# Ranking the expert gates in two halves, and visiting every expert twice

## The chip, the core and the metric

The kernel runs on one core of a Trainium2 chip. The metric is the device time in microseconds of one execution, as the median of several. The engines are named as in the profile: PE (TensorE matmul), PEld (its weight loads), DVE (VectorE), ACT (ScalarE), POOL (GpSimd, which here also issues all indirect DMAs) and SP (SyncE, which issues most other DMAs).

## What is computed

A layer norm without weights, then attention with low-rank query and key projections and a causal mask, and beside it a mixture of experts in which each expert picks its tokens. Both are added to the input. The arrays are float32: 16 batches, 512 tokens, 256 channels; 16 heads of 16 channels; 8 experts with 512 hidden channels, each taking 128 tokens of every batch.

```
xn = layernorm(x)
q, k = (xn @ q_a) @ q_b, (xn @ k_a) @ k_b        # per head, rank 64
v = xn @ v_w.T + v_b
y = softmax(causal(q @ k.T / 4)) @ v @ o_w.T + o_b
probs = softmax(xn @ choice_w.T)                 # over the 8 experts
G, I = top_k(swap(probs), 128)                   # per batch and expert: 128 tokens
h = silu(xn[I] @ w1[e])
out = zeros.at[I].add(G * (h @ w2[e]))
result = x + y + out
```

## The kernel before

**Attention stage.** The work is cut into 64 slots, one for four heads of one batch (`G = 4*b + g`), each of ten units `t`. `slot_steps` writes down, for a slot, which steps stand at which unit; every engine walks the same list in the same order and does its own part of each step, waiting on semaphores. A slot computes `score` of slot G+3 (PE, then a row maximum on DVE, line 719), `scoret` of slot G+1 (PE, `exp` on ACT line 565, causal mask on POOL line 469) and `pv` of slot G (PE line 908; the copy `yraw` on ACT line 569 comes once per slot, so its start marks the slots). `PROJECTIONS` puts the work for later batches between them: `xload` and `lnstat` (the load of `xln`, then its statistics on DVE, line 657), `xt`, `qk` and `mid` (projections, split into three bf16 parts on ACT, DVE line 588 `rest` and POOL, then stacked by twelve DMAs of SP for the scores of the batch two later), `v`, `o`, and `xres` (SP loads x again into `xres`, POOL adds the bias, line 477). Pairs of batches 1 to 6 run in a hardware loop, the first and last pair stand as straight code.

**Routing.** `routing_steps` puts the gates at the end. When the logits of all 16 batches are there (slot 56), DVE and ACT make the softmax of [128, 4, 16, 8] values; PE transposes them, so that 128 partitions are the pairs (batch, expert) with 512 tokens each. Then DVE draws the 128 largest of each row by 47 operations in a chain (`RANK_OPS`: `max` of eight, `max_index`, `match_replace`; lines 633 to 637), 5 to 8 of them in each of slots 57 to 63. `rows` turns the places into row numbers, `rowst` transposes back, and POOL gathers the tokens of the first two groups by eight indirect DMAs. Scratch for this lies in `xn` and `xln`, free by then.

**Expert stage.** It is a second block of instructions, begun when all engines have ended the first. A group is one expert and four batches (`GB4`); there are 32 groups `n = 4*e + grp`, and the weights of an expert are loaded and split into a high and a low part once (`w` on ACT line 1070, `w_low` on DVE line 1089). A group is: gather of 4 x 128 rows (POOL line 961), `pick` (PE transposes, split on ACT and DVE line 1094), `h` (PE line 1141, silu on ACT line 1078, split on DVE lines 1098 and 1100), `down` (PE line 1157, product with the gate on DVE line 1109 into `mixed`), and four scatter-adds into the output (POOL line 1049). POOL's order is gather of group n+2, scatter of group n-1, gather of group n+3, and so on; the scatter of a group waits until that of the group four back has landed.

## Time and profile before

| | |
|---|---|
| Time, 3 runs | 1301.11, 1294.84, 1301.05 us; median 1301.05 |
| Profiled execution, its own time | 1295.71 us |
| Its span in the trace | 1293.8 us |
| Mean granted TensorE clock | 0.969 |
| Busy: PE, DVE, POOL, ACT | 1184.1, 967.2, 692.0, 668.7 us |
| Attention stage | 0 to 861 us |
| Expert stage | 861 to 1294 us |

Busy times are sums over both stages, which have different limits. A matmul's end is modelled, so a PE that is always busy is not PE at its peak. A row of the timeline gives the start, the duration, the engine and line, and in brackets how long the engine was idle before and what it then waited for.

### The profile page before, as it was taken

How to read it: one execution, taken by the hardware profiler on the slowest of the kernel's cores; microseconds unless marked ns; L12 is line 12 of the kernel's file. 1: busy time of each engine (PE TensorE's matmuls, PEld its weight loads, DVE VectorE, ACT ScalarE, POOL GpSimd, SP SyncE). 2: the span in 40 equal slices, each digit the busy share in tenths (PEclk: the TensorE clock that was granted, in tenths of full speed). 3: DMA queues.
4: the chain of work that ended last, by engine and by line, in shares of the span. 5: the costliest groups of instructions: out<-in, count | busy, mean ns of one | idle time of the engine just before them, and what ended most of it. 6: DMA issues, size and time to landing. Idle time of an engine off the chain costs nothing. (4 is left out here: it accounts for less than half of the span.)

```text
span 1293.8 us, 29459 instructions
## 1 busy us (share of the span) xinstructions
PE 1184.1 (92%) x8502; PEld 819.8 (63%) x8502; DVE 967.2 (75%) x3293; ACT 668.7 (52%) x1312; POOL 692.0 (53%) x1021
## 2 busy tenths in 40 slices
PE   6799999999999999999999998769999999999995
PEld 5545555555555555555555553348988888888885
DVE  3588888879889888888888879935666666666662
ACT  2357667667667677677667665522332323233320
POOL 1235344355355355345345443344888888888885
PEclk9779999999999999999999999979999999999998
DMA  5443443443443443443444342132555555556454
GB/s 141 114 116 83 116 116 100 116 116 98 115 115 98 115 115 99 115 115 100 113 115 112 100 99 67 34 114 38 111 99 95 114 93 102 94 100 109 85 78 53
DMA packets 106287, 130.31 MB, mean 101 GB/s; under 512 B 21580, under 2 KB 75476, under 8 KB 106196
## 3 DMA queue, kind: packets, MB, share of 16 engines
q1 hardware_dynamic: 76356, 94.46, 28.1%
q0 software_dynamic: 24576, 33.57, 15.6%
q10 hardware_dynamic: 5264, 1.32, 0.5%
q8 instruction: 27, 0.44, 0.1%
q14 instruction: 64, 0.52, 0.1%
HBM read 44.84 MB, written 33.55 MB: 61 GB/s over the span
## 5 line engine op out<-in xcount | busy, mean ns | idle before, releaser
L719 DVE CUSTOM_DVE_ANT_0 junk<-bank,rowmask 128x256 bf16<-128x256 f32 (+3 forms) x1024 | 454.9, 485 | 60.3 <-PE bank L866 38.0
L565 ACT ACTIVATE probs<-bank 128x512 f32<-128x512 f32 x640 | 377.3, 598 | 158.0 <-PE bank L887 143.8
L469 POOL TENSOR_SCALAR_AFFINE_SELECT probs<-probs 128x256 f32<-128x256 f32 (+1 forms) x640 | 224.2, 363 | 311.0 <-ACT probs L565 308.9
L866 PE MATMUL bank<-kstk,qstk 96*128 96x256 bf16 (+3 forms) x1024 | 250.7, 306 | 34.3 <-DVE rowmax L719 17.3
L887 PE MATMUL bank<-qstk,kstk 98*128 98x256 bf16 (+3 forms) x1024 | 251.0, 307 | 3.8 <-ACT probs L565 2.6
L1049 POOL DMA_INDIRECT out_rows<-mixed,rows x128 | 208.9, 1632 | 58.2 <-issue 38.1
L1078 ACT ACTIVATE hid<-bank 128x512 f32<-128x512 f32 x128 | 76.6, 598 | 228.5 <-PE bank L1141 228.5
L908 PE MATMUL bank<-probs,vaug 128*32 128x512 f32 (+3 forms) x2048 | 168.5, 448 | 6.6 <-POOL probs L469 6.6
L1157 PE MATMUL bank<-w_hi,hid_hi 128*128 128x256 f32 x512 | 147.3, 288 | 0.0
L1157 PE MATMUL bank<-w_hi,hid_lo 128*128 128x256 f32 x512 | 144.9, 283 | 0.0
L1157 PE MATMUL bank<-w_lo,hid_hi 128*128 128x256 f32 x512 | 144.8, 283 | 0.0
L866 PEld LDWEIGHTS bank<-kstk,qstk 96*128 96x128 bf16 x1024 | 89.7, 100 | 79.5 <-DVE rowmax L719 38.3
L887 PEld LDWEIGHTS bank<-qstk,kstk 98*128 98x128 bf16 x1024 | 76.7, 99 | 99.2 <-issue 48.0
L1109 DVE TENSOR_SCALAR mixed<-bank,gate_sel 128x256 f32<-128x256 f32 x128 | 56.1, 480 | 92.0 <-PE bank L1157 92.0
L908 PEld LDWEIGHTS bank<-probs,vaug 128*32 128x32 f32 x2048 | 54.1, 110 | 95.9 <-issue 74.1
L460 POOL TENSOR_TENSOR qk_part<-rest,qk_part 128x512 bf16<-128x512 f32 x64 | 74.6, 1166 | 58.0 <-ACT qk_part L541 55.1
L1157 PEld LDWEIGHTS bank<-w_lo,hid_hi 128*128 128x128 f32 x512 | 98.2, 192 | 0.0
L1157 PEld LDWEIGHTS bank<-w_hi,hid_hi 128*128 128x128 f32 x512 | 98.2, 192 | 0.0
L1157 PEld LDWEIGHTS bank<-w_hi,hid_lo 128*128 128x128 f32 x512 | 98.1, 192 | 0.0
L1098 DVE CAST hid_hi<-hid 128x512 fp32r<-128x512 f32 x128 | 56.9, 445 | 48.7 <-ACT hid L1078 47.1
L1100 DVE TENSOR_TENSOR hid_lo<-hid,hid_hi 128x512 fp32r<-128x512 f32 x128 | 89.2, 697 | 4.4
L719 DVE DVE_READ_ACCUMULATOR2_ANT rowmax<- 128x1 f32 x1024 | 84.8, 83 | 0.0
(131 smaller groups left out, 2097.8 us busy)
## 6 DMA issues: line engine op xcount, KB each, us to landing
qstk<-qk_part SPq DMA_DIRECT2D x96, 256.0 KB, 4.8
kstk<-qk_part SPq DMA_DIRECT2D x96, 256.0 KB, 4.7
xln<-in_L_attn_hidden_states SPq DMA_DIRECT2D x16, 512.0 KB, 6.1
xn_rows<-xn SPq DMA_DIRECT2D x16, 512.0 KB, 2.8
xres<-in_L_attn_hidden_states SPq DMA_DIRECT2D x16, 512.0 KB, 3.6
out_rows<-xres SPq DMA_DIRECT2D x16, 512.0 KB, 2.9
qstk<-in_L_ffn_w SPq DMA_DIRECT2D x8, 512.0 KB, 4.0
kstk<-in_L_ffn_w SPq DMA_DIRECT2D x8, 512.0 KB, 3.9
```

The costliest lines, as they stand in the source:

```text
L460: nc.gpsimd.tensor_tensor(qk_part[2][:, k, :], rest[k % 2][:], qk_part[1][:, k, :], ALU.subtract).then_inc(lo_done, 1)
L469: nc.gpsimd.affine_select(out=block, in_=block, compare_op=ALU.is_ge, fill=0.0, base=0, pattern=[[0, len(cols)], [1, P]], channel_multipli ...
L565: nc.scalar.activation(probs[n % 2][:, 512 * k:512 * k + 512], SCORET[k % 2][:], ACT.Exp, scale=SCALE).then_inc(exp_done, 1)
L719: last = nc.vector.tensor_tensor_reduce(out=junk[k % 2][:, col:col + width], in0=SCORE[score_bank(UN * n + k)][:, col:col + width], in1=ro ...
L866: last = nc.tensor.matmul(SCORE[score_bank(UN * n + k)][:, col:col + width], qstk[b % 2][0:KS, GH * g + h, P * i:P * i + P], kstk[b % 2][0 ...
L887: last = nc.tensor.matmul(SCORET[k % 2][:, col:col + width], kstk[b % 2][0:KS + SHIFT, GH * g + h, P * j:P * j + P], qstk[b % 2][0:KS + SH ...
L908: last = nc.tensor.matmul(Y[2 * HD * h:2 * HD * h + 2 * HD, P * k:T], vaug[b % 2][:, k, GH * g + h, :], probs[n % 2][:, col:col + width], ...
L1049: nc.gpsimd.indirect_dma_start(out=out_rows, out_offset=bass.IndirectOffsetOnAxis(ap=moe.rows[:, GB4 * grp + j, e:e + 1], axis=0), in_=mix ...
L1078: nc.scalar.activation(hid[k % 2][:], UP[k][:], ACT.Silu).then_inc(silu_done, 1)
L1098: nc.vector.tensor_copy(hid_hi[n % 2][:, k, :], hid[k % 2][:]).then_inc(hid_high, 1)
L1100: nc.vector.tensor_tensor(hid_lo[n % 2][:, k, :], hid[k % 2][:], hid_hi[n % 2][:, k, :], ALU.subtract).then_inc(hid_done, 1)
L1157: last = nc.tensor.matmul(DOWN[k][:, D * t:D * t + D], a, b, start=m == 0, stop=m == len(todo_mm) - 1)
```

## The change

The gates are ranked in two halves of eight batches. For the first half, softmax, transpose and ranking stand in slots 28 to 55, two ranking operations in each of slots 30 to 53 (at units 2 and 4), on 64 partitions of 512 tokens. The second half has its softmax and transpose in slots 57 and 58, and its 47 ranking operations go into the expert stage: four in each of the first twelve groups. The scratch has tiles of its own.

An expert is now visited once for each half, with two groups at a visit: 16 visits, each of which loads and splits the expert's weights. A scatter waits for the one two groups back. The gathers of the first two groups are issued by POOL in slots 59 to 61 (`fetch`). The bias add on POOL becomes a step of its own (`xadd`), in the same place but for the last batch, where it stands after the last causal masks. Only the second and third pair of batches still run as a loop; the rest, and DVE and SP in the expert stage, stand as straight code.

```diff
+PER_VISIT = HB // GB4
+VISITS = 2 * E
+LOOPED = 3
...
-RANK_PLACES = {7: (4, 5, 6, 8, 9), 6: (0, 1, 3, 4, 6, 7), 5: (0, 1, 3, 4, 6, 7), 4: (0, 1, 3, 4, 6, 7),
-               3: range(8), 2: range(8), 1: range(8)}
+RANK_PLACES = (2, 4)
+RANK_FIRST = 30
...
+    for half, gates in enumerate((28, NG - 7)):
+        if G == gates:
+            out += [(5, ("gate_max", half, 0)), (6, ("gate_max", half, 1)), (7, ("gate_exp", half, 0)),
+                    (8, ("gate_norm", half, 0)), (9, ("gate_norm", half, 1))]
+        if G == gates + 1:
+            out += [(0, ("gate_norm", half, 2)), (2, ("rankt", half, 0))]
...
+    done = len(RANK_PLACES) * (G - RANK_FIRST)
+    if 0 <= done < RANK_OPS:
+        out += [(t, ("rank", done + m, 0)) for m, t in enumerate(RANK_PLACES) if done + m < RANK_OPS]
...
+    if 3 <= NG - G <= 5:
+        first = 3 * (5 - (NG - G))
+        out += [(t, ("fetch", *divmod(first + m, GB4))) for m, t in enumerate((1, 4, 7)) if first + m < 2 * GB4]
...
-    return [("yt", B - 1, 0), ("rowst", 0, 0), ("gather", 0, 0), ("gather", 1, 0), ("yt", B - 1, 1)] \
+    return [("xadd", B - 1, 0), ("yt", B - 1, 0), ("gather", 0, 0), ("gather", 1, 0), ("yt", B - 1, 1)] \
...
+def expert_steps(body):
...
+        n = EG * body + grp
+        v, second = divmod(n, PER_VISIT)
+        if n == RANK_GROUPS:
+            out.append(("rowst", 1, 0))
         out += [("h", n, ft) for ft in range(FT)]
+        if second and v + 1 < VISITS:
+            out += [("w", v + 1, 0), ("w_low", v + 1, 0)]
...
+        out += [("rank", n, 0)] * (n < RANK_GROUPS)
+        for j in range(GB4 // 2):
+            out += [("down", n - 1, j)] * (n >= 1) + [("rank", n, 1)] * (n < RANK_GROUPS and j == 0)
+        if n == RANK_GROUPS - 1:
+            out.append(("rows", 1, 0))
+        if not second and v >= 1:
+            out += [("w", v, 1), ("w_low", v, 1)]
...
+def place_of(n):
+    v, second = divmod(n, PER_VISIT)
+    half, e = divmod(v, E)
+    return HB * half + GB4 * second, e
```

Where instructions stand, engine by engine. DVE in the attention stage, the second slot of a batch, before (`stats` is the last `lnstat`, `junk,rowmax` are pieces of the row maxima of `score`):

```order
L657 BN_STATS stats<-xln 128x6 x2
L663 BN_AGGR meanvar<-stats 128x2 x4
L719 ISA junk,rowmax<-bank,rowmask 128x256
L719 ISA rowmax 128x1
L719 ISA junk,rowmax<-bank,rowmask 128x256
L719 ISA rowmax 128x1
L756 TENSOR_TENSOR xres<-bank,xres 128x256
L719 ISA junk,rowmax<-bank,rowmask 128x512
```

And the same place of the changed kernel, in a slot from 30 to 53:

```order
L729 ISA junk,rowmax<-bank,rowmask 128x256
L729 ISA rowmax 128x1
L766 TENSOR_TENSOR xres<-bank,xres 128x256
L1004 MAX top<-ranked 64x8
L729 ISA junk,rowmax<-bank,rowmask 128x512
L729 ISA rowmax 128x1
L729 ISA junk,rowmax<-bank,rowmask 128x384
L729 ISA rowmax 128x1
L729 ISA junk,rowmax<-bank,rowmask 128x128
L729 ISA rowmax 128x1
L1006 MAX_INDEX top_at<-top,ranked 64x8
```

Two ranking operations now stand between the row maxima of each of these slots; nothing else moved there.

POOL at the end of the attention stage, before (`probs` are causal masks, `xres` the bias add of the last batch, the DMAs the first gathers):

```order
L477 TENSOR_TENSOR xres<-xres,ob_all 128x1024
L469 AFFINE_SELECT probs<-probs 128x2x128
L469 AFFINE_SELECT probs<-probs 128x128
L469 AFFINE_SELECT probs<-probs 128x2x128
L469 AFFINE_SELECT probs<-probs 128x128
L469 AFFINE_SELECT probs<-probs 128x2x128 x2
L469 AFFINE_SELECT probs<-probs 128x128
L469 AFFINE_SELECT probs<-probs 128x2x128
L961 DMA qstk<-xn_rows,rows 128x256 x4
L961 DMA kstk<-xn_rows,rows 128x256 x4
```

And after (the last of the eight single gathers, in slot 61, down to the end of the stage):

```order
L988 DMA kstk<-xn_rows,rows 128x256
L486 AFFINE_SELECT probs<-probs 128x128
L486 AFFINE_SELECT probs<-probs 128x2x128 x2
...
L486 AFFINE_SELECT probs<-probs 128x128
L486 AFFINE_SELECT probs<-probs 128x2x128
L494 TENSOR_TENSOR xres<-xres,ob_all 128x1024
```

The last bias add went behind the last masks, and the gathers went two slots forward.

DVE in the expert stage, before, a group behind which the next expert's `w1` is split:

```order
L1089 TENSOR_TENSOR w_lo<-qstk,w_hi 128x1024
L1093 REGISTER_ALU
L1094 TENSOR_TENSOR pt_lo<-bank,pt_hi 128x512
L1093 REGISTER_ALU
L1094 TENSOR_TENSOR pt_lo<-bank,pt_hi 128x512
L970 ISA
L970 COPY gate_sel<-gates 128x4
L1104 REGISTER_ALU
L1109 TENSOR_SCALAR mixed<-bank,gate_sel 128x256 x4
```

And after, the first such group:

```order
L1135 TENSOR_TENSOR w_lo<-qstk,w_hi 128x1024
L1158 TENSOR_TENSOR pt_lo<-bank,pt_hi 128x512 x2
L996 COPY gate_sel<-gates 128x4
L1006 MAX_INDEX top_at<-top,ranked 64x8
L1007 MATCH_REPLACE ranked<-top,ranked 64x512
L1173 TENSOR_SCALAR mixed<-bank,gate_sel 128x256 x2
L1004 MAX top<-ranked 64x8
L1006 MAX_INDEX top_at<-top,ranked 64x8
L1173 TENSOR_SCALAR mixed<-bank,gate_sel 128x256 x2
```

Two ranking operations stand ahead of each half of `mixed`, and such a group with a `w_lo` now comes every second time instead of every fourth.

## Rows read from the trace of the kernel before

**Rows 1.** The page: busy sums, and POOL's 40 slices in tenths.

```profile
PE 1184.1 (92%) x8502; PEld 819.8 (63%) x8502; DVE 967.2 (75%) x3293; ACT 668.7 (52%) x1312; POOL 692.0 (53%) x1021
POOL 1235344355355355345345443344888888888885
```

**Rows 2.** The page: the chain that ended last, by engine.

```profile
POOL 23%; issue 6%; PE 3%; DMA 0%; DVE 0%; ACT 0%; POOLq 0%
```

**Rows 3.** Busy by window, expert stage: PE, PEld, DVE, ACT, POOL, then clock, DMA.

```profile
888.00:1263.00 375.00, 358.46 (x2339) 322.08 (x2338) 239.51 (x450) 113.78 (x188) 305.43 (x229) 1.00 0.54 97
```

**Rows 4.** Busy by window, one batch in mid attention: two slots, one, one.

```profile
604.30:629.40 25.10, 23.37 (x186) 13.86 (x185) 20.17 (x84) 17.08 (x39) 10.30 (x23) 1.00 0.62 143
629.40:640.50 11.10, 11.03 (x96) 7.07 (x97) 10.74 (x46) 7.41 (x14) 2.50 (x7) 1.00 0.37 121
640.50:652.00 11.50, 11.50 (x85) 6.25 (x84) 10.08 (x42) 8.47 (x17) 9.08 (x17) 1.00 0.10 30
```

**Rows 5.** Timeline of DVE where a batch turns over.

```profile
609.92 0.69 DVE L588 TENSOR_TENSOR rest<-bank,qk_part 128x512 f32<-128x512 f32 x1
623.41 0.43 DVE L657 BATCH_NORM_STATS2 stats<-xln 128x6 f32<-128x256 f32 x1 [2.07 <-DMA xln<-in_L_attn_hidden_states]
657.70 0.69 DVE L588 TENSOR_TENSOR rest<-bank,qk_part 128x512 f32<-128x512 f32 x1
```

**Rows 6.** Busy by window: the two parts of that batch's turn.

```profile
609.90:623.40 13.50, 11.85 (x99) 7.24 (x98) 9.94 (x40) 9.11 (x22) 5.03 (x12) 1.00 0.71 165
623.40:657.70 34.30, 34.15 (x269) 20.01 (x269) 31.11 (x130) 23.94 (x47) 16.86 (x35) 1.00 0.33 91
```

**Rows 7.** Timeline of DVE: a value load; a MAX8 and its follower.

```profile
824.79 0.08 DVE L635 MATCH_VALUE_LOAD xn<-xn,xln 128x8 f32 x1
...
827.07 0.69 DVE L633 MAX8 xn<-xln 128x8 f32<-128x512 f32 x1
827.67 0.41 DVE L756 TENSOR_TENSOR xres<-bank,xres 128x256 f32<-128x256 f32 x1
```

**Rows 8.** Busy by window: slots 56 and 57; 58 and 59; 60; 61 to 63.

```profile
747.50:775.30 27.80, 25.68 (x190) 14.27 (x188) 21.54 (x86) 18.09 (x40) 9.73 (x22) 0.94 0.48 111
775.30:801.10 25.80, 21.38 (x157) 9.70 (x158) 24.84 (x97) 13.08 (x25) 9.17 (x21) 0.93 0.26 84
801.10:813.10 12.00, 9.11 (x74) 4.19 (x75) 11.72 (x48) 6.98 (x14) 3.90 (x11) 1.00 0.01 2
813.10:843.60 30.50, 22.47 (x183) 10.84 (x181) 26.22 (x76) 15.73 (x29) 10.71 (x25) 0.89 0.11 36
```

**Rows 9.** Busy by window of line 776 alone (`qk`): PE, PEld; two slots.

```profile
629.40:652.00 22.60, 4.94 (x15) 2.61 (x15) 1.00 0.23 75
```

**Rows 10.** Timeline of the handover, 831 to 861 us, single rows.

```profile
834.81 2.35 POOL L477 TENSOR_TENSOR xres<-xres,ob_all 128x1024 f32<-128x1024 f32 x1 [5.39 <-ACT probs L565]
839.75 3.80 PE L908 MATMUL bank<-probs,vaug 128*32 128x512 f32 x32 [5.13 <-POOL probs L469]
855.11 0.38 SPq L412 DMA_DIRECT2D out_rows<-xres  x1
857.39 0.94 POOL L961 DMA_INDIRECT kstk<-xn_rows,rows  x1 [0.30 <-issue]
860.85 1.94 PE L1125 MATMUL bank<-ident,qstk 128*128 128x128 f32 x8 [6.37 <-PEq L218]
```

**Rows 11.** Timeline of POOL and DVE where an expert's weights are split.

```profile
1027.25 1.02 POOL L961 DMA_INDIRECT qstk<-xn_rows,rows  x1 [0.30 <-issue]
...
1029.30 1.23 DVE L1089 TENSOR_TENSOR w_lo<-kstk,w_hi 128x1024 fp32r<-128x1024 f32 x1 [0.28 <-ACT w_hi L1070]
1029.87 1.48 POOL L961 DMA_INDIRECT qstk<-xn_rows,rows  x1 [0.30 <-issue]
...
1040.88 1.02 POOL L961 DMA_INDIRECT kstk<-xn_rows,rows  x1 [0.30 <-issue]
...
1053.55 1.02 POOL L961 DMA_INDIRECT qstk<-xn_rows,rows  x1 [0.31 <-issue]
```

More of the change, by code:

```diff
@@ L158, in __init__ @@
         self.out_stored = out_stored
+        self.ranked = ranked
+        self.top = top
+        self.top_row = top_row
+        self.top_at = top_at
+        self.first = first
 def build(nc, x, q_a, q_b, k_a, k_b, v_w, v_b, o_w, o_b, choice_w, w1, w2, out):
@@ L174, in build @@
     U_PAIR, S_PAIR = 48, 16
-    for i in range(1, PAIRS - 2):
+    for i in range(1, LOOPED - 1):
         for s, z in zip(pair_steps(i), pair_steps(i + 1)):
@@ L213, in build @@
             gathered=[sem(f"gathered{g}") for g in range(EG)],
-            out_stored=sem("out_stored"))
+            out_stored=sem("out_stored"),
+            ranked=[keep(f"ranked{u}", [HALF, T], fp32) for u in range(2)],
+            top=keep("top", [HALF, CAP], fp32), top_row=keep("top_row", [HALF, CAP], fp32),
+            top_at=keep("top_at", [HALF, CAP], u32), first=keep("first", [P, 1], fp32))
         banks = [ctx.enter_context(nc.psum_tensor(f"bank{i}", [P, 512], fp32)) for i in range(8)]
@@ L304, in build @@
             out_stored = moe.out_stored
-            gate_step = sem("gate_step")
+            gate_step = [sem(f"gate_step{half}") for half in range(2)]
             bias_step = sem("bias_step")
@@ L947, in expert_steps @@
             out += [("pick", n + 1, dt) for dt in range(DT)]
-        if n + 2 < E * EG:
+        if n + 2 < EG * E:
             out.append(("gather", n + 2, 0))
-        if n >= 1:
-            out += [("down", n - 1, j) for j in range(GB4 // 2)]
-        if grp == 0 and e >= 1:
-            out += [("w", e, 1), ("w_low", e, 1)]
-    return out + [("down", n, j) for j in range(GB4 // 2) if e == E - 1]
-def gather(nc, moe, xn_dram, n):
-    e, grp = divmod(n, EG)
-    for j in range(GB4):
-        nc.gpsimd.indirect_dma_start(
-            out=moe.picked[grp][:, j, :], out_offset=None, in_=xn_dram,
-            in_offset=bass.IndirectOffsetOnAxis(ap=moe.rows[:, GB4 * grp + j, e:e + 1], axis=0)).then_inc(moe.gathered[grp], 16)
@@ new lines, in expert_steps, with gather, select @@
+    return out + [("down", n, j) for j in range(GB4 // 2) if body == E - 1]
+def place_of(n):
+    v, second = divmod(n, PER_VISIT)
+    half, e = divmod(v, E)
+    return HB * half + GB4 * second, e
+def gather(nc, moe, xn_dram, n, j):
+    first, e = place_of(n)
+    nc.gpsimd.indirect_dma_start(
+        out=moe.picked[n % EG][:, j, :], out_offset=None, in_=xn_dram,
+        in_offset=bass.IndirectOffsetOnAxis(ap=moe.rows[:, first + j, e:e + 1], axis=0)).then_inc(moe.gathered[n % EG], 16)
+def select(nc, moe, n):
+    first, e = place_of(n)
+    nc.vector.tensor_copy(moe.gate_sel[n % EG][:], moe.gates[:, first:first + GB4, e:e + 1]).then_inc(moe.sel_done, 1)
@@ L973, in experts, with rank, by_be @@
+def rank(nc, moe, n):
+    r, op = divmod(n, 3)
+    a, z, eight = moe.ranked[r % 2], moe.ranked[(r + 1) % 2], slice(8 * r, 8 * r + 8)
+    if op == 0:
+        return nc.vector.max(moe.top[:, eight], a[:])
+    if op == 1:
+        return nc.vector.max_index(moe.top_at[:, eight], moe.top[:, eight], a[:])
+    return nc.vector.match_replace(z[:], moe.top[:, eight], a[:], -1.0)
+def by_be(t, half):
+    return t[:, HB * half:HB * half + HB, :].rearrange("p b e -> p (b e)")
 def experts(nc, sem, ident, banks, moe, xn_dram, out_rows):
@@ L1005, in experts, with whole @@
         added = [sem(f"added{g}") for g in range(EG)]
+        rank_step, rows_ready, rows_in, gates_in = sem("rank_step"), sem("rows_ready"), sem("rows_in"), sem("gates_in")
+        same = lambda value, per_body: value
+        def whole(steps_fn):
+            steps_fn(start_steps + [s for body in range(E) for s in expert_steps(body)], same)
         def program(eng, steps_fn):
-            same = lambda value, per_expert: value
+            turn = RANK_GROUPS // EG
             steps_fn(start_steps + expert_steps(0), same)
-            with eng.Fori(1, E - 1) as e:
-                steps_fn(expert_steps(1), lambda value, per_expert: e * per_expert + (value - per_expert))
+            with eng.Fori(1, turn) as i:
+                steps_fn(expert_steps(1), lambda value, per_body: i * per_body + (value - per_body))
+            steps_fn(expert_steps(turn), same)
+            with eng.Fori(turn + 1, E - 1) as i:
+                steps_fn(expert_steps(turn + 1), lambda value, per_body: i * per_body + (value - (turn + 1) * per_body))
             steps_fn(expert_steps(E - 1), same)
```

229 lines of the change are left out of this document (117 added, 112 removed), and 2 rows, old and new, of the table PROJECTIONS.

## The prediction

> **What bounds the kernel now.** I read the page first. Its busy sums call PE the bound, at 92%, but they are averages over two stages. The slices of POOL in [rows 1] show the two: half busy or less in the attention stage, 8 tenths in all of the expert stage. The chain that ended last names POOL with 23% and "issue" with 6% of the span in [rows 2].
>
> The windows of the expert stage settle it. From 888 to 1263 us POOL is busy 305.4 of 375.0 us with 229 instructions [rows 3]. Each has about 0.3 us of issue ahead of it [rows 11], 229 x 0.3 = 68.7 us, and 305.4 + 68.7 = 374.1. POOL never waits there. A group costs it four gathers and four scatters, about 13 us, so this stage is as long as POOL's list, counted from the first scatter.
>
> In the attention stage I read windows cut at the slots. One batch takes 25.1 + 11.1 + 11.5 = 47.7 us, of which PE is busy 45.9 and DVE 41.0; in the third slot DVE has 0.4 us to spare, in the fourth 1.4 [rows 4]. The timeline shows a turn of fixed length in it: from the last `rest` of a batch at 609.92 to the statistics at 623.41, which waited 2.07 us for the load of `xln` queued behind the stacking DMAs, is 13.5 us; from there to the next such `rest` at 657.70 is 34.3 us [rows 5]. In the 34.3 us DVE is busy 31.1, so it has 3.2 us of idle time; in the 13.5 us it is busy 9.9 [rows 6].
>
> The end of the attention stage is bound by DVE, with the ranking: 24.8 busy of 25.8 us in slots 58 and 59, 11.7 of 12.0 in slot 60 [rows 8]. After that comes a handover in which little runs: the bias add on POOL at 834.81, after a wait of 5.39 us, holds the last masks, and with them PE for 5.13 us; the gathers need the finished ranking, so the last is issued at 857.39 and the expert stage's first matmul starts at 860.85 [rows 10].
>
> **The change part by part.** The sum is made against the profiled execution's own time, 1295.7 us (span 1293.8, about 2 us around it). The median of the runs shown is 1301.05; I carry the difference over to that.
>
> (a) *Ranking leaves slots 57 to 63: -19 us.* What would these slots take without it? Slots 58 and 59 belong to a batch with no projections for a later one. The pair of slots that answers to them takes 11.1 + 11.5 = 22.6 us with PE full [rows 4], and 4.94 us of it are the 15 `qk` matmuls that fall away [rows 9]: 17.7. DVE's 20.8 us of work there lose the `rest` and `xn` pieces too, so it is no tighter. Against 25.8 now [rows 8] that is -8.1. Slot 60 is 12.0 and would be some 9.7 with the next batch's projections gone: -2.3. Slots 61 to 63 have no scores; they now take 30.5 together (the last of it held up by the bias add, whose wait is gone because it stands behind the masks) and I take 24.5: -6.0. Slots 56 and 57 take 27.8 now against a normal 25.1; they lose some projections and keep half of the softmax, so I take 25.0: -2.8. Sum -19.2. The bounds are -11, where the slots stay at the length of normal ones, and -24. The eight fetches lie on POOL at slots 59 to 61: 8 x 1.25 = 10 us (0.94 and 0.3 of issue [rows 10]) on an engine busy 9.2 of 25.8 us [rows 8]. Behind a fetch wait the masks, and behind these `pv`; a mask of 0.3 to 0.4 us comes about once in 1 us, so a delay of 1.25 is worked off within two. I cost them at nothing, at worst 3.
>
> (b) *Handover: -5 us.* The block ends with its slowest engine, now POOL at 858.33; 2.5 us later PE starts. Without the gathers the last is SP's issue of the final store at 855.11 [rows 10], so -3; the transposes and copies of `rowst` in between, and PE's lowered clock (0.89 on average from 813 to 844 [rows 8], where it waited for POOL) give perhaps 2 more, with 1 to 5 as bounds. The first groups may also see the full clock sooner, for which I take -1.5, an estimate between 0 and 3.
>
> (c) *First half's ranking in slots 30 to 53: +12 us.* A ranking operation put between others costs 0.60 us (a MAX8, from its start to that of its follower), and the two other kinds 0.08 more for their value load [rows 7]: 0.65 on average, on all partitions or half of them alike, since time goes by the 512 tokens. Two per slot are 1.3 us. Six of the 24 slots fall in the 13.5 us stretches, where DVE waits 2.07 us for the load anyway: hidden, and if that cover were gone, 8 us. The other 18 add 18 x 1.3 = 23.4 us to the stretches of 34.3 us, six in number, with 3.2 us of idle each, 19.2 in all. If all of it can be used the cost is 4; if none, 23. Slots 58 to 60 show that DVE can run with 2 to 4% idle [rows 8], 1.2 us of 37, so 2 us a stretch are usable: 23.4 - 12 = 11.4. PE is nearly full in the stretches, which it is not in slots 58 to 60; I take 12. Behind DVE wait PE's next scores (three banks) and the shared banks of the projections.
>
> (d) *First half's softmax in slots 28 and 29: +1.5.* Five operations of half size and a transpose; bounds 0.5 and 4.
>
> (e) *Eight more visits: +5.5 us.* PE and ACT have the room. POOL has none. Where the low part of `w1` is made on DVE (1.23 us), the gather under it takes 1.48 us instead of 1.02, and POOL's group is 13.6 us long (1027.25 to 1040.88) where the next is 12.7 (to 1053.55) [rows 11]. Part of that 0.9 is the place in the pattern; at 0.7 each, 8 x 0.7 = 5.5; bounds 0 and 8. The scatter's wait for the one two groups back has a whole group's POOL time between, some 13 us, against a landing of 2 to 4: no cost.
>
> The Trainium skill, SBUF — State Buffer, section "Who interferes with whom", has it that a DVE operation with two SBUF inputs competes only with GpSimd's reads and, by inference there, not with the writing of descriptors. By that rule this term would be 0. The row speaks against it.
>
> (f) *Second half's ranking in twelve groups: +1; first scatter later: +2.* DVE is busy 239.5 of 375 us [rows 3], 8.3 of 13 per group. Four operations are 2.6 us, the second split every other group 0.6 more: 11.5 of 13. POOL stays the bound, and what DVE delays is hidden behind its list, except before the first scatter, where a split (1.2) and two to four ranking operations now stand ahead of the first `mixed`.
>
> (g) *Straight code instead of loops: 0.* Slots of the first pair, which is straight code today, last as long as those in the loop; the extra wait at the loop's end is taken out of the wait for the load in [rows 5].
>
> Sum: -19.2 - 5 - 1.5 + 12 + 1.5 + 5.5 + 3 = -3.7 us. From 1295.7 that is 1292.0; from the median, 1297.
>
> **The rivals.** *Better hidden (chance 0.26).* The ranking in mid attention fills DVE's idle time almost whole: (c) is 5 rather than 12, the change -11, time 1290. For it: DVE ran 98% full in slot 60. Against: PE is full there as well, and DVE's idle time lies late in the stretch.
>
> *No cost of splits (0.10).* The lengthened gather is due to the weight's DMA or to chance, (e) is 0, and the change is -9.2: 1292. The rule of the Trainium skill named above would give this. The boundary in [rows 11] repeats at the other experts, so I hold it unlikely.
>
> *DVE sets the pace in mid attention (0.17), the one on the other side.* No idle time is usable, since in-order PE stalls on the shared banks as soon as DVE lags; (c) is 23 and the change is +7: 1308. It is slower than before as soon as (c) is over 16.
>
> *The expert stage becomes DVE's (0.07).* In a group with a split, the last `hid_lo` of PE's `h` is followed on DVE by 1.2 + 1.4 + 0.2 + 2.6 + 1.8 = 7.2 us, after 5.4 of `h`: 12.6 beside POOL's 12.9. If waits add 1 us to each of twelve groups: +12 - 3.7 = +8, 1309.
>
> *The end doesn't shrink (0.05).* Masks and `pv` hold slots 58 to 63 near their present length, (a) is -11: +4.5, 1305.
>
> That leaves 0.35 for the forecast itself, with a range of its own of 1292 to 1302.
>
> **How the numbers follow.** What a measurement can tell from no change is about 0.5%, 6.5 us. Faster than 1294.5 are the first two rivals, 0.36. Slower than 1307.6: the third and fourth but for a part of each, 0.20. Within: 0.44. The range goes to the better-hidden case with a larger (a) below, and to the case on the other side above: 1283 to 1311.
>
> **What would show it.** Windows over four slots between 30 and 53: 49.7 us a batch by (c) (48.5 if well hidden, 51.5 if not), DVE over 95% busy. Slots 58 and 59: 17 to 18 us together. From the last `yraw` to the first `pick` about 12 us. The expert stage from first matmul to the end: 441 us against 433 now, with POOL still without waits, and gathers of 1.4 us at every second group. I would be wrong if POOL waited for `mixed` there, or if the slots with ranking took over 13 us each.

## The result, and the profile after

The changed kernel takes 1318.91 us in the median of 4 runs (1313.63 to 1322.76), the kernel before 1297.94 beside it (4 runs): a ratio of 1.016, with an interval of 1.011 to 1.021. It is slower, and by more than the range of the forecast allowed. The profiled execution has a span of 1311.9 us (own time 1313.6).

The page of the changed kernel: busy sums, PE's granted clock in 40 slices, the packets that bring code (the queue named `instruction`; 0.92 MB in 56 packets are 16 KB each), and the group in which PE waits for the stacking DMAs.

```profile
PE 1190.9 (91%) x8508; PEld 822.1 (63%) x8508; DVE 1010.2 (77%) x3396; ACT 686.4 (52%) x1330; POOL 696.9 (53%) x1021
PEclk9879999999999999998999999989999999999998
q8 instruction: 56, 0.92, 0.3%
L877 PE MATMUL bank<-kstk,qstk 96*128 96x256 bf16 (+3 forms) x1024 | 254.6, 311 | 39.1 <-DMA kstk<-qk_part 30.1
```

The same page of the kernel before has this row of code packets:

```profile
q8 instruction: 27, 0.44, 0.1%
```

To see where the time went I compared the starts of the `yraw` copies, one per slot, of both traces. At the copy of slot 55 the changed kernel is 35.0 us behind (first row before, second after). By slot 63 it has won 14.0 back, by the first `pick` of the expert stage another 6.1, it loses 0.4 until the first scatter and 2.8 from there to the last: 35.0 - 14.0 - 6.1 + 0.4 + 2.8 = 18.1, the difference of the spans. So the end and the handover shrank by 20.1 of the 25.7 us that I had for them, and mid attention cost 35 us where 13.5 stood in the sum.

```profile
747.52 0.60 ACT L569 ACTIVATE yraw<-bank 128x512 f32<-128x512 f32 x1 [0.44 <-PE bank L908]
782.53 0.60 ACT L587 ACTIVATE yraw<-bank 128x512 f32<-128x512 f32 x1 [0.44 <-PE bank L919]
```

Of the 35.0 us, 5.9 had come by slot 27, 3.8 came in slots 28 and 29, where the first half's softmax stands, and 25.4 in slots 30 to 55.

I call the stretch from the last `rest` of a batch to the statistics its turn, as in [rows 5], and number it by the batch, counted from 0, whose pieces are stacked in it. The turn of batch 12, which answers to [rows 6], by windows: from the statistics to the last `rest`, from there to the next statistics (the turn), and the 3.4 us from just before its end; then slots 56 and 57, 58 and 59, 60, and 61 to 63, as in [rows 8]. The columns are those of [rows 3].

```profile
595.27:633.63 38.36, 37.33 (x272) 20.88 (x272) 34.49 (x140) 24.19 (x47) 16.93 (x35) 0.94 0.30 81
633.63:648.43 14.80, 12.13 (x100) 7.48 (x99) 10.80 (x45) 9.20 (x22) 5.02 (x12) 0.98 0.67 153
648.00:651.40 3.40, 3.40 (x18) 1.49 (x21) 2.83 (x12) 1.65 (x4) 0.41 (x1) 0.52 0.00 0
...
782.50:809.30 26.80, 24.84 (x186) 14.25 (x185) 18.72 (x78) 17.32 (x38) 9.23 (x22) 0.94 0.49 109
809.30:831.50 22.20, 19.45 (x161) 9.95 (x162) 18.58 (x81) 13.38 (x26) 10.32 (x22) 1.00 0.34 103
831.50:840.40 8.90, 8.57 (x74) 4.05 (x73) 8.34 (x38) 6.73 (x13) 6.37 (x14) 1.00 0.17 49
840.40:864.60 24.20, 20.62 (x183) 10.72 (x182) 7.83 (x29) 15.43 (x29) 15.03 (x30) 1.00 0.21 66
```

Both parts of the batch grew: 38.4 us against 34.3 and 14.8 against 13.5 [rows 6]. DVE is not full, it idles 3.9 of the 38.4 us, so it is not the rival in which DVE sets the pace. And the clock stands at 0.52, the lower of its two levels (1.2 GHz), for those 3.4 us. Ahead of that PE had waited for the stacking DMA, on PE's timeline:

```profile
647.10 0.38 PE L877 MATMUL bank<-kstk,qstk 96*128 96x512 bf16 x1 [2.55 <-DMA kstk<-qk_part]
```

In the kernel before this wait is 1.5 us in every other batch and nothing in the rest (only the weight load ahead waits, 0.2 to 0.4 us), with no fall of the clock from 338 to 768 us. The changed kernel has waits of 1.8 to 3.0 us in the eight turns of batches 7 to 14 and nine falls, one in each batch from 388 to 801 us.

### The profile page after: what moved, and what is told of

It is laid out like the page before. It is cut to its first block and busy times, and to the rows that moved or that the text cites. A ratio compares the mean times of both kernels' runs of the same rounds, so it can differ in the third digit from the quotient of the medians.

```text
span 1311.9 us, 27293 instructions
## 1 busy us (share of the span) xinstructions
PE 1190.9 (91%) x8508; PEld 822.1 (63%) x8508; DVE 1010.2 (77%) x3396; ACT 686.4 (52%) x1330; POOL 696.9 (53%) x1021
## 5 line engine op out<-in xcount | busy, mean ns | idle before, releaser
L729 DVE CUSTOM_DVE_ANT_0 junk<-bank,rowmask 128x256 bf16<-128x256 f32 (+3 forms) x1024 | 453.7, 483 | 47.8 <-PE bank L877 39.5
L877 PE MATMUL bank<-kstk,qstk 96*128 96x256 bf16 (+3 forms) x1024 | 254.6, 311 | 39.1 <-DMA kstk<-qk_part 30.1
L898 PE MATMUL bank<-qstk,kstk 98*128 98x256 bf16 (+3 forms) x1024 | 255.3, 312 | 4.2 <-DMA qstk<-maxrow 2.4
L988 POOL DMA_INDIRECT qstk<-xn_rows,rows x64 | 69.9, 1092 | 30.9 <-issue 18.1
L1213 PE MATMUL bank<-pt_hi,w_hi 128*128 128x512 f32 x256 | 80.5, 396 | 4.0 <-DVE pt_lo L1158 4.0
```

What stands on the lines that cost most here:

```text
L729: last = nc.vector.tensor_tensor_reduce(out=junk[k % 2][:, col:col + width], in0=SCORE[score_bank(UN * n + k)][:, col:col + width], in1=ro ...
L877: last = nc.tensor.matmul(SCORE[score_bank(UN * n + k)][:, col:col + width], qstk[b % 2][0:KS, GH * g + h, P * i:P * i + P], kstk[b % 2][0 ...
L898: last = nc.tensor.matmul(SCORET[k % 2][:, col:col + width], kstk[b % 2][0:KS + SHIFT, GH * g + h, P * j:P * j + P], qstk[b % 2][0:KS + SH ...
L988: nc.gpsimd.indirect_dma_start(out=moe.picked[n % EG][:, j, :], out_offset=None, in_=xn_dram, in_offset=bass.IndirectOffsetOnAxis(ap=moe.r ...
L1213: last = nc.tensor.matmul(UP[k][:], a[:, dt, f], b[:, dt, :], start=m == 0 and dt == 0, stop=m == 2 and dt == DT - 1)
```

## The experiments

Two things of the change touch every batch in mid attention: the ranking on DVE, and the code, written out where there was a loop. The packets of code doubled. The first runs take these two apart.

**Code alone.** The kernel before, with the loop of the attention stage kept for pairs 1 and 2 only.

```diff
-                with eng.Fori(1, PAIRS - 1) as i:
+                with eng.Fori(1, LOOPED) as i:
...
-                steps_fn(pair_steps(PAIRS - 1) + epilogue_steps(), same)
+                steps_fn([s for i in range(LOOPED, PAIRS) for s in pair_steps(i)] + epilogue_steps(), same)
```

> The kernel before with one edit: only pairs 1 and 2 of the attention run as a loop, the rest is straight code, as in the changed kernel; no other instruction is added or moved. If straight code is a cause (theory S: the code that must be fetched delays the last stacking DMAs, PE's wait for them grows from 1.5 to about 2.6 us, and its clock then halves for 3.4 us), the turn from the last rest to the statistics is 14.3 us or more instead of 13.5 in batches 7 to 13, a batch takes 50 to 50.5 us instead of 47.8, and the time is 12 to 20 us longer. If the ranking alone is the cause (theory R), the time is within 4 us of before and the turn stays 13.5 us.

Measured: 1312.88 us, ratio 1.012 (1.009 to 1.016). Written-out code costs 16 us with nothing else changed; the run has 50 packets of 16 KB instead of 27 (an expectation below says 29 more, which is the changed kernel's number). The turns of batches 7, 9, 10, 11 and 14 grew and their last transfer came late (batch 8's grew too, 14.9 us, with a packet 11.4 us in and the last transfer in time); those of 12 and 13, which I had expected to grow too, did not. Two batches of this run, by windows; they do the same work:

```profile
623.50:671.30 47.80, 45.44 (x362) 26.70 (x362) 40.40 (x166) 32.70 (x68) 21.95 (x47) 1.00 0.44 112
522.80:573.00 50.20, 47.00 (x356) 27.06 (x355) 39.46 (x161) 32.07 (x66) 20.66 (x46) 0.93 0.38 97
```

The first is as short as a batch of the looped kernel, so written-out code isn't slow in every batch. What differs is a packet. These are the DMA queues from 4 to 12 us into the turn, in the slow batch (526.8 to 534.8 us) and, behind the dots, in the good one (627.5 to 635.5), and PE's wait behind each:

```profile
q1 hardware_dynamic: 1050, 1.76, 98.4%
q8 instruction: 1, 0.02, 1.1%
q10 hardware_dynamic: 34, 0.01, 0.7%
...
q1 hardware_dynamic: 1079, 1.79, 100.3%
q10 hardware_dynamic: 34, 0.01, 0.7%
```

```profile
536.65 0.58 PE L867 MATMUL bank<-kstk,qstk 96*128 96x512 bf16 x1 [2.92 <-DMA kstk<-qk_part]
...
635.89 0.38 PE L867 MATMUL bank<-kstk,qstk 96*128 96x512 bf16 x1 [1.52 <-DMA kstk<-qk_part]
```

**Load alone.** The loop kept, and two MAX8 of 64x512 that nothing depends on in each of slots 8 to 55.

```diff
+    if 8 <= G < 56:
+        for t in (2, 4):
+            put[t].append(("load", G, t))
...
+                        elif kind == "load":
+                            nc.vector.max(spare[:, 8 * (k // 4):8 * (k // 4) + 8], rowmask[0:64, :])
```

> The kernel before, with two MAX8 of 64 x 512 put into units 2 and 4 of each of slots 8 to 55, on DVE, of data that nothing else uses; the loop stays. They stand for the ranking operations, 1.2 us a slot. Theory R (DVE's load alone lengthens the turn and brings the clock down): a batch takes over 50 us and the time is 25 us longer or more over 12 batches. Theory S: the turn stays 13.5 us, the loop's clock stays 1.0, and each batch is longer only by what DVE cannot hide, 1.5 to 2.5 us, in all 18 to 30 us; the turn from rest to statistics tells the two apart.

Measured: 1314.67, ratio 1.016 (1.014 to 1.018). The two parts of a batch:

```profile
584.67:621.04 36.37, 35.43 (x276) 20.47 (x275) 34.29 (x136) 24.58 (x48) 17.39 (x36) 1.00 0.32 86
621.04:634.23 13.19, 11.47 (x96) 6.95 (x95) 10.94 (x42) 8.85 (x21) 5.04 (x12) 1.00 0.70 164
```

Eight operations of 0.6 us make a batch 1.5 us longer, 49.4 instead of 47.8 on average over slots 16 to 51, in the part ahead of the turn; the turn is no longer, and the clock doesn't fall. By the whole time, 19.6 us in twelve batches, it is 1.6. For the six batches of the real ranking that is 9 to 10 us.

**Both.** Written-out code, and the same load in slots 30 to 53.

> The kernel before with both edits: straight code from pair 3 on, and two MAX8 in each of slots 30 to 53. It is the changed kernel's mid attention without its other parts. If straight code and load explain the loss there, the 55th yraw starts 30 to 36 us later than in the kernel before, and e1 gives what of it is the code. If it is later by under 20, something else of the change (the softmax in slot 28, the tiles' places) takes the rest.

Measured: 1317.41, ratio 1.017 (1.014 to 1.020). From code alone it is 4.5 us, about half of 9. That the whole time is the change's own is chance, for this run hasn't the 20 us that the change wins behind slot 55. Its copy of slot 55 starts 19.5 us behind the kernel before, where the changed kernel is 35.0 behind:

```profile
766.97 0.60 ACT L574 ACTIVATE yraw<-bank 128x512 f32<-128x512 f32 x1 [0.44 <-PE bank L915]
```

This is under the 20 that I had set as the mark, so code and load give 19.5 of the 35.0 us and something else of the change goes with 15.5. By stretches: 3.0 against 5.9 up to slot 27, 0.7 against 3.8 in slots 28 and 29, so that the softmax costs some 3 us, and 15.7 against 25.4 from slot 30 on. There the traces differ in where the packets fall: this run has four late turns (batches 7, 9, 10, 11) with four falls of the clock, the changed kernel six with nine. Its turns without a packet are longer too (below). How much each of these takes of the 9.7 us isn't told apart.

**The clock.** The changed kernel, with 8 matmuls that nothing reads ahead of PE's wait for the stacking DMAs (from batch 7 on, in a free score bank).

```diff
+                            if g == 0 and k == 0 and n >= 24:
+                                for _ in range(8):
+                                    nc.tensor.matmul(SCORE[score_bank(UN * n + k)][:], wqk_hi[:, 0, 0:P], wqk_hi[:, 0, :],
+                                                     start=True, stop=True)
                             if g == 0 and k == 0:
                                 pe.wait_ge(stacked[b % 2],
```

> The changed kernel, with eight matmuls of 512 columns (1.8 us) on PE ahead of its wait for the stacking DMAs, once for each batch from 7 on, into the score bank that is free then; their results are overwritten. If the length of PE's idle wait is what brings the clock down, the clock stays 1.0 through slots 28 to 60 and each of the eight batches is 1.5 us or so shorter: 10 to 14 us in all, near 1303. If the clock falls for another reason, or the wait is not what costs, the time stays within 3 us of the changed kernel or grows.

Measured: 1306.48, 12.4 us less than the changed kernel's median. Each against its own runs of the kernel before, ratios of 1.010 (1.007 to 1.013) and 1.016, it is some 8, so I take 8 to 12. From 380 to 780 us its clock is 1.00 (first row), that of the changed kernel 0.96 (second):

```profile
380.00:780.00 400.00, 384.78 (x2968) 228.28 (x2966) 352.29 (x1429) 265.06 (x546) 175.19 (x374) 1.00 0.43 106
380.00:780.00 400.00, 371.32 (x2806) 215.10 (x2805) 343.82 (x1390) 256.70 (x524) 169.63 (x361) 0.96 0.41 102
```

The turns stayed at 13.8 to 15.0 us, so the falls of the clock are a cost beside the late transfers, some 0.9 to 1.4 us for each of the nine. The same 8 matmuls in the written-out kernel before:

> The kernel before with all code written out, and 8 matmuls of 512 columns into a free score bank ahead of PE's wait for the stacking transfers, from slot 24 on, so that PE does not idle there. It parts the cost of written-out code (1.2%, 16 us) into the falls of the clock and the rest. Theory F: four falls in mid attention at 1.5 us each, as the same matmuls gave back some 12 us for eight or nine falls in the changed kernel: -5 to -7 us against the first experiment, a clock without falls between 340 and 780 us; the last transfers stay late by 1 us in the same turns. Rival K (the clock carries all of it): -14 us or more, back to the kernel before.

Measured: 1304.99 (ratio 1.006, 1.004 to 1.008), 7.9 us less than code alone. Half of the cost of the code is the clock. Late transfers are a large part of the rest: in the profiled run of code alone the turns of batches 7 to 14 sum to 113.7 us against 108.2 before, and each batch with a late turn is longer by some 2 us or more. The parting isn't clean, since the added matmuls moved the packets as well: here eight turns of batches 4 to 14 are late instead of five.

**Which engine's code.** Code written out on one engine, the loop kept on the others.

```diff
+                if eng in (nc.vector,):
+                    steps_fn([s for i in range(1, PAIRS) for s in pair_steps(i)] + epilogue_steps(), same)
+                    return
```

> The kernel before, with VectorE's code alone written out for all pairs of batches and the loop kept on the other engines. With all engines written out the median rose by 1.2%, and 29 more instruction packets came in mid attention. Theory F (a packet of code that is fetched while the stacking transfers run delays the last of these; PE's wait grows from 1.5 to some 2.6 us; the clock falls to half for 3.4 us after it): the packets are those of all engines together, so VectorE alone brings a part of them (some 10, by its share of the rows written out), the turns without a packet stay at 13.5 us, and the time rises by 2 to 6 us. Rival V (written-out code costs where VectorE itself runs it, whatever is fetched): nearly the whole 16 us come back. Rival P (it costs where PE runs it): 0.

> The kernel before, with PE's code alone written out for all pairs and the loop kept on the other engines. Theory F: PE has the most instructions, so most of the 29 added packets are its own, the turn is 14 us or more in those batches where a packet falls among the stacking transfers and 13.5 in the others, each of the former with a fall of the clock and some 3 us; +6 to +14 us in all. Rival V (VectorE's own written-out code costs): 0. Rival P (it costs where PE runs it, in all batches alike): +12 to +16 us spread evenly, with no falls of the clock.

Measured: 1300.86 for VectorE (ratio 1.005, 1.003 to 1.007), 1307.89 for PE (1.008, 1.006 to 1.011). Together they are some 18 us, about the whole. The added 16 KB packets are PE's: its run has 56, that of VectorE 27 as before. What VectorE's run changed are the 8 KB packets of another queue, q14, in their places, and to 46 from 64 rather than, as I had expected, to more of them. In PE's run the turns of batches 9, 11, 13 and 14 land late, at 13.5 to 13.9 us, with packets 4.5 to 5.9 us into the turn, and the other seven of batches 4 to 14 at 12.3 to 12.5. Only the last of the four has a fall of the clock, where I had expected one in each: so a late transfer costs without it, some 2 us in each of those batches. In VectorE's run two of these eleven turns had a packet of q14 among the stacking transfers (7.7 and 7.8 us into the turn), and only these two landed late, at 13.2 and 13.4 us.

**Moving the packets.** Is the packet the cause, or only there? The written-out kernel before, and 64 matmuls of 32 columns on PE ahead of a score, which shift all later packets.

```diff
+                            if n == 16 and k == 0:
+                                for _ in range(64):
+                                    nc.tensor.matmul(SCORE[score_bank(UN * n + k)][:, 0:32], wqk_hi[:, 0, 0:P], wqk_hi[:, 0, 0:32],
+                                                     start=True, stop=True)
```

> The kernel before with all code written out (as the first experiment), and 64 matmuls of 32 columns more on PE ahead of the scores of slot 16, which nothing reads. They are some 128 instructions of PE, half of the 256 that a 16 KB packet of code holds, so all later packets of PE's code come half a period, about 8 us, earlier beside the work. Theory F (a packet fetched in the stacking turn delays the last stacking transfer and PE): in the run without them the turns of batches 9, 10 and 11 had a packet 10 us into the turn and their last transfer landed after 13.1 to 13.7 us instead of 12.3. With the shift these three go back to 12.4 us, and batches 12 and 13, whose packets came just after the turn, at 12.5 to 13.5 us, get them at 4 to 6 us and land after 13 us or more. Rival C (the long turns belong to these places of the written-out code for another reason, such as the order of the semaphores or the batches' data): batches 9 to 11 stay late and 12 and 13 stay at 12.3. The time in all stays within 5 us of the first experiment's 1312.9.

Measured: 1323.91. The place lies in a step that the remaining loop runs twice, and the matmuls cost 21 us there, so the total says nothing. The turns do. The packets came 7 to 11 us earlier. Those of batches 10, 12 and 13 came 2 to 3 us into the turn, before the transfers; I had expected the last two at 4 to 6 us, and that half of the expectation wasn't tested. The last transfers of batches 7, 10, 11 and 14 went from 13.2 to 13.7 us to 12.3 to 12.5, batch 9 stayed at 13.0 with an 8 KB packet of q14 7.5 us into its turn. PE's wait in batch 10, 2.92 us above:

```profile
552.21 0.38 PE L871 MATMUL bank<-kstk,qstk 96*128 96x512 bf16 x1 [1.55 <-DMA kstk<-qk_part]
```

From slot 33 to slot 55 code alone had lost 9.4 us to the looped kernel; this run loses 0.6. The same shift in the changed kernel, placed where PE waits for its first data, in two sizes:

```diff
                 pe.wait_ge(ident_done, 1)
+                pe.wait_ge(consts, 3)
+                for _ in range(64):
+                    nc.tensor.matmul(SCORE[0][:, 0:8], ident_bf[:], ident_bf[:, 0:8], start=True, stop=True)
```

> The changed kernel, with 64 matmuls of 8 columns (bf16) at PE's very beginning, where it otherwise waits for its first data until 8 us; nothing reads them. They are 128 instructions, half of a 16 KB packet of code, and do nothing else but shift where the packets of PE's code fall in the slots: some 8 us earlier. In the changed kernel's trace a packet came 7 to 10 us into the turn in batches 7 to 12, the last stacking transfer landed after 13.3 to 13.8 us, and the clock fell once in every batch. Theory F: with the shift these packets come at about 1.5 us into the turn, before the transfers, the last lands after 12.7 us, most of the falls are gone, and the kernel is 8 to 14 us faster than the changed one (some 1306 to 1311). Rival C (written-out code and the ranking are slow there whatever the packets do): the changed kernel's 1318.9, within 3 us.

> The same with 32 matmuls in place of 64: a shift of some 4 us. Theory F: the packets that came at 7 to 10 us into the turn come at 3 to 6 us, still among the stacking transfers, and those of batches 13 and 14, which came at 13.1 us, come at 9; so all eight turns are late, and the time is the changed kernel's 1318.9 or up to 4 us more. Rival C: the same as with 64. Rival W (any matmuls at the start help, by the clock or by the order of things): as fast as with 64.

Measured: 1308.87 with 64 (ratio to the kernel before 1.011, 1.009 to 1.012), 1320.58 with 32 (1.019, 1.017 to 1.021). So 64 matmuls without use win 10 us by the medians and 7 by the ratios, and 32 win nothing; between the two runs, measured beside each other, are 11.7 us. With 32 the trace has slots 30 to 55 1.6 us shorter than in the changed kernel but reaches slot 7 5.9 us later (with 64: 5.4 shorter and 4.0 later), for which I have no reason. With 64 no packet of PE's is left among the transfers of batches 7 to 14 and seven of these eight turns land at 12.6 to 12.8 us; the eighth, 13.3, has a packet of q14. With 32 the shift was larger than I had reckoned: four turns have their packet at 2.4 to 2.9 us and are good, and the other four, with packets at 6.5 to 10.2 (one of them of q14), late. One step failed: with 64 the clock still fell in each of batches 9 to 14 of the profiled run (which, with 1316.1 us, was the slowest of the five), behind waits of 1.8 to 2.5 us, such as this one, with no packet from 1.9 to 12.0 us into the turn:

```profile
643.75 0.38 PE L880 MATMUL bank<-kstk,qstk 96*128 96x512 bf16 x1 [2.00 <-DMA kstk<-qk_part]
```

Over all 17 traces there are 187 turns (batches 4 to 14). In 42 a code packet starts 6.2 to 10.7 us into the turn: their last transfer lands after 13.0 us or more. In 135 none starts from 3.9 to 10.7 us: all land at 12.0 to 12.9 but one, 13.3, whose packet came at 3.8. The 10 between (3.9 to 6.2 us) are of both kinds. These bounds I drew after seeing the turns; the runs that moved the packets are the test, the count is not.

**A loop for the others.** The changed kernel, with pairs 4 and 5 as a loop on all engines but DVE.

> The changed kernel, with slots 32 to 47 (batches 8 to 11) as a loop of two turns on all engines but VectorE, where the ranking makes the two turns differ. The other engines have the loop's code by its second turn, batches 10 and 11. Theory F: in batches 10 and 11 few packets of code come, the turn falls from 14.7 to 13.6 us, the clock holds, and the two batches are 49 us long instead of 51; batches 8, 9 and 12 to 14 stay as they were. In all -3 to -7 us against the changed kernel. Rival R (the ranking itself lengthens the turn and the wait): batches 10 and 11 stay at 51 us, 0 in all.

Measured: 1316.58, the changed kernel's time within its spread. The loop's second round holds the turns of batches 12 and 13. They had no packet of PE's among the transfers and landed at 12.8, as in theory F, but were 14.7 and 14.0 us long instead of 13.6, one with a fall of the clock, and the two batches took 52.7 and 51.0 us, not 49. And in the turn of batch 11, where the loop goes round, POOL stood for 6.4 us and ACT for 3.4 with nothing that the trace shows as a cause:

```profile
587.32 0.29 POOL L492 TENSOR_SCALAR_AFFINE_SELECT probs<-probs 128x128 f32<-128x128 f32 x1 [6.37 <-issue]
```

**The bias add alone.** The kernel before, with `xadd` of the last batch at the start of the epilogue.

> The kernel before, with only the bias add of the last batch moved on GpSimd from slot 61 to behind the last causal masks, as in the changed kernel. In the kernel before PE waited 5.13 us for masks that stood behind this add, and the end of the attention stage needs the ranking as well, which lies on VectorE. If the wait of PE was on the path: -3 to -5 us from slot 63 on, of which the handover may take back the time of the add itself (some 2 us), because the store needs it. If the ranking on VectorE alone sets the end: 0.

Measured: 1290.27, ratio 0.997 (0.995 to 0.999): PE's wait of 5.13 us [rows 10] is 1.31, and this one edit gives 4 to 5 us, a fifth to a quarter of the 20 that the end and the handover gave the change.

```profile
829.77 2.37 POOL L477 TENSOR_TENSOR xres<-xres,ob_all 128x1024 f32<-128x1024 f32 x1
829.86 3.95 PE L908 MATMUL bank<-probs,vaug 128*32 128x512 f32 x32 [1.31 <-POOL probs L469]
```

**The splits.** The kernel before, and a subtraction of the size of a split in the second group of each expert.

```diff
+        out += [("spare", n, 0)] * (grp == 1)
...
+                    if kind == "spare":
+                        nc.vector.tensor_tensor(spare[:], w_hi[0][:], w_lo[0][:], ALU.subtract)
```

> The kernel before, and in the second group of each of the eight experts one more subtraction of the size of a low half of w1 on VectorE, of two tiles of SBUF into a third that nothing reads. My forecast had 0.7 us for each such subtraction, by the gathers beside it that take 1.48 instead of 1.02 us. If so: +5.6 us (0.4%), with a gather of some 1.4 us in each such group. By the changed kernel's own trace, where the expert stage grew by 2.8 us after its first scatter: +2.5 to +3. By the rule that such operations don't touch the writing of descriptors: 0.

Measured: 1294.78, ratio 0.9995 (0.998 to 1.001): nothing. But it fell beside scatters, which take 1.73 us there against 1.62 on average elsewhere, and not beside gathers, so it didn't test the row that the forecast went by.

**What stands against the kernel before.** `xadd` moved, and matmuls without use where PE idles between the stages.

```diff
+                            if n == B - 1 and k == 0:
+                                idle_matmuls(5)
...
                 program(pe, steps)
+                idle_matmuls(20)
...
+                            if n in (0, 1):
+                                for _ in range((5, 8)[n]):
+                                    nc.tensor.matmul(DOWN[0][:], w1_hi[:, 0, 0:P], w1_hi[:, 0, :], start=True, stop=True)
```

> The kernel before with the bias add of the last batch moved behind the last masks (1290.3 us, -0.33%, by itself), and matmuls that nothing reads where PE idles between the stages: 5 ahead of the last output projection, 20 behind it, 5 and 8 ahead of the first two groups' first layer. In the trace PE's clock is at half in 836 to 843 and 846 to 860 us, where the output projection takes 4.4 us instead of some 3 and the first group's first layer 8 instead of 5.6. If the clock stays at full: another -3 to -4 us, 1287. If POOL's gathers set the start and the first groups of POOL's list hide the rest: 0 to -1.

Measured: 1286.71, ratio 0.993 (0.991 to 0.995), faster than both kernels. From the last `yraw` to the first scatter the clock is 0.92 (first row), where it is 0.77 with `xadd` alone, and the stretch is 3.9 us shorter:

```profile
834.70:875.60 40.90, 35.09 (x184) 28.45 (x185) 23.75 (x50) 12.76 (x20) 16.65 (x17) 0.92 0.28 90
833.90:878.70 44.80, 30.36 (x146) 25.48 (x147) 22.34 (x46) 12.98 (x20) 15.37 (x16) 0.77 0.27 82
```

The changed kernel with all of these edits:

> The changed kernel with everything that the runs so far gave: the 64 matmuls at the start, 8 ahead of PE's wait for the stacking transfers from batch 7 on (they gave back 12 us), and those between the stages (they gave 3.6 us in the kernel before). If the three add up: 1318.9 - 12 - 6 - 3 = 1298; the first two share the falls of the clock, so the second gives only the transfers' 1 us in some six turns. Theory F has 1296 to 1300, so the halves still don't beat the kernel before, 1295, because the ranking in mid attention costs 1.5 us per batch in six batches and the lasting rest is 1 us or so per written-out batch. If the halves were good once the packets are out of the way: under 1291.

Measured: 1312.69 (1305.63 to 1321.88, ratio 1.012, 1.006 to 1.019). They don't add up; even its fastest run is behind the kernel before, so theory F's 1296 to 1300 missed. With the clock held in batches 7 to 14 and one late turn of these eight left, slots 30 to 55 still take 16.8 us more than before, of which the load is 9 to 10. In the profiled run, 1318.6 us, PE stood for 5.1 us where the first loop goes round:

```profile
284.81 0.61 PE L909 MATMUL bank<-qstk,kstk 98*128 98x512 bf16 x1 [5.08 <-issue]
```

## Why the prediction was wrong

(g) *Straight code: 0.* This step failed. It was argued from slots of the first pair lasting as long as looped ones. That reading was wrong: the two turns in that straight code (batches 2 and 3, at 126 and 176 us) take 14.1 and 13.8 us against 13.5 in the loop, and PE waits 2.1 and 1.9 us there against 1.5, the first time with a fall of the clock at 139.6. None of the rows in front showed it, the trace did:

```profile
139.24 0.38 PE L866 MATMUL bank<-kstk,qstk 96*128 96x512 bf16 x1 [2.14 <-DMA kstk<-qk_part]
```

Straight code costs 16 us in the kernel before. The mechanism, shown by moving the packets: a packet of code among the stacking transfers delays the last of these by 0.7 to 1.5 us. The turn is a chain with no slack, and PE's longer wait behind it often, not always, goes with a fall of the clock for 3.4 us. That the delay is about the packet's own 0.9 to 1.4 us, during which it holds one of the 16 DMA engines (1.1% of 16 engines' 8 us is 1.4 us), fits, but is argued.

(c) and (d) *Mid attention: +13.5.* With (g) at 0, it was 35.0. By the run with both, code and load are 19.5 of it and the softmax (d) some 3, twice its 1.5. The load alone is 9 to 10 by the looped run, so (c) was sized 2 to 3 too high. The other 12 to 13 us stay open between the places of the packets, the longer turns without one, and the batches before slot 28. Seen the other way, by effects: load 9 to 10, the falls of the clock 8 to 12 by the run with warm PE, and the eight turns of batches 7 to 14, which sum to 116.9 us where eight of 13.5 are 108, 9 more. These can overlap and aren't a sum. The rival with (c) at 23 had the right sign for another reason: DVE had idle time left in every stretch.

(a) *The end: -19.2.* It was -14.0. Slots 60 to 63 came out as worked out (33.1 against 34.2 us). Slots 58 and 59 take 22.2 instead of 17.7: PE alone is busy 19.45 us there, more than I left after taking `qk` off, and it waits for the rest. Slots 56 and 57 take 26.8 instead of 25.0, with a fall of the clock in them (0.94).

(b) *Handover: -6.5 with the clock.* -6.1, right. Of this and the end together 3.7 us are `xadd` alone, in the trace of its run.

(e) and (f) *Expert stage: +8.5.* It was +3.3, and (e) was mis-sized, on a wrong reading of [rows 11]: the `w_lo<-kstk` there is the split of `w2`, not of `w1`. A second split of `w1` falls beside scatters and costs nothing, at a second split of `w2` a gather takes 0.4 more. These are that place on POOL and DVE in the changed kernel:

```profile
1070.26 0.98 POOL L988 DMA_INDIRECT qstk<-xn_rows,rows  x1 [0.30 <-issue]
1071.55 1.84 POOL L988 DMA_INDIRECT qstk<-xn_rows,rows  x1 [0.31 <-DMA out_rows<-mixed,rows]
...
1071.35 1.22 DVE L1135 TENSOR_TENSOR w_lo<-kstk,w_hi 128x1024 fp32r<-128x1024 f32 x1 [0.28 <-ACT w_hi L1116]
```

Gathers beside such a split and the `hid` work are 12 with 1.40 us on average in the changed kernel and 6 with 1.37 before, others take 0.99: 6 x 0.4 = 2.4, and one more of 1.66, make about the 2.8 measured. POOL never waited but for 2.7 us at the last group (2.9 before), as forecast. The Trainium skill, SBUF — State Buffer, "Who interferes with whom", would have the split at 0. The run with the spare subtraction agrees in its time. So do two gathers that lie beside such a split alone, both 0.95 us, here the second:

```profile
1019.18 0.95 POOL L988 DMA_INDIRECT qstk<-xn_rows,rows  x1 [0.30 <-issue]
...
1019.17 1.27 DVE L1135 TENSOR_TENSOR w_lo<-kstk,w_hi 128x1024 fp32r<-128x1024 f32 x1
```

The long gathers begin under the split and go on beside the cast to `hid_hi` behind it. What lengthens them isn't shown, so they don't speak against the rule, though the prediction took [rows 11] to do so.

The terms against the trace: 5.2 for (a), 0.4 for (b), 21.5 for (c), (d) and (g), -5.2 for (e) and (f) are 21.9, from the forecast's -3.7 to the measured +18.2.

## What to carry to other kernels

Before a loop is written out, look for the chain in it that has no slack and ends in a DMA: in this kernel code then came by DMA all the time, 56 packets of 16 KB instead of 27, and where one met that transfer the chain grew by 0.7 to 1.5 us. The tell-tales are more packets on the instruction queues, a period of bad iterations among good ones with the same work, and a time that changes when instructions without use are added at the start. Where PE waits 2 us in each iteration, price the clock as well as the wait, and try matmuls without use in the wait. When a run stands for a part of the change, compare it with the change over the same stretch and not by the whole time. And take the parts of a change that are good by themselves: the bias add and the warm handover won 8 us in the kernel before, more than the whole change promised.

## What the hardware showed unexpectedly

- A run of 64 matmuls of 32 columns on PE, with no wait in it, went with the lower clock level for its 14 us: 0.2 us for each matmul.

```profile
240.00:254.00 14.00, 14.00 (x69) 11.99 (x72) 3.20 (x14) 1.56 (x4) 0.41 (x1) 0.51 0.01 2
```

- Waits of 1.5 us in the looped kernel went with no fall of the clock but one (at 334 us), and most waits of 1.8 to 2.1 us in the changed one and its variants with one. A wait of 3.06 us had one; one of 2.50 us, with VectorE's code alone written out, and one of 2.58 us, in the written-out kernel ahead of the first batch with added matmuls, had none: the length of the wait doesn't decide alone, and what does stays open.
- In turns without a packet the last transfer lands at 12.7 us in the changed kernel and at 12.4 before, with equal bytes. Why stays open too; the tiles lie at other addresses, but that wasn't tried.
- In two of the 17 profiled runs one or two engines stood for 3 to 6 us where a loop goes round, with "issue" as all that the trace names. The other runs pass such places without it. The reason is open.
